# GNN edge and node kernel on one core: the destination rows of a group of 512 edges come as five blocks of 128 rows in one transfer, and five matmuls pick them where eight did

## The reference, cut to what matters

```python
row, col = edge_index[0], edge_index[1]          # src, dst; both of 50000 edges, dst is sorted
edge_input = concatenate([x[row], x[col], edge_attr], axis=-1)   # 128 + 128 + 16 columns
h    = silu(edge_input @ eW1 + eb1)
m_ij = silu(h @ eW2 + eb2)
agg  = segment_sum(m_ij, row, num_segments=50000)
update = silu(concatenate([x, agg], -1) @ nW1 + nb1) @ nW2 + nb2
out  = layernorm(x + (x + update))
```

## Time and profile before

| | |
|---|---|
| median of three runs | 1586.3 us |
| profiled execution: time, span | 1574.37 us, 1572.9 us |
| TensorE / GpSimd / VectorE / ScalarE busy | 77% / 66% / 48% / 29% of the span |
| DMA, mean over the span | 224 GB/s |
| granted TensorE clock, mean | 0.914 of full |

### The profile page before, as it was taken

One profiled execution on the slowest core, in us unless ns is written; L12 is line 12 of the kernel. 1 busy time (PEld: TensorE's weight loads), 2 busy tenths in 40 slices (PEclk: granted clock), 3 DMA queues, 4 the chain that ended last, 5 costly groups with the idle time before them and its releaser, 6 DMA issues.

```text
span 1572.9 us, 24119 instructions
## 1 busy us (share of the span) xinstructions
PE 1207.4 (77%) x6825; PEld 865.5 (55%) x6825; DVE 761.0 (48%) x2819; ACT 459.5 (29%) x846; POOL 1041.8 (66%) x1267
## 2 busy tenths in 40 slices
PE   3812677788787888878888877777778979999994
PEld 3711354555554555545545454544445569888884
DVE  8940343443434434344343333333333449888885
ACT  0000111222222222222222222211212247777774
POOL 8877466556565565555656565666566548999996
PEclk9985799899999999998999898989889889999998
DMA  9995444456666666566656556555545259999994
GB/s 376 410 408 204 123 126 140 145 172 200 183 185 190 186 195 182 186 192 181 192 177 200 170 172 183 172 172 172 165 147 176 62 197 410 412 412 413 410 408 167
DMA packets 175498, 352.94 MB, mean 224 GB/s; under 512 B 30350, under 2 KB 81855, under 8 KB 175364
## 3 DMA queue, kind: packets, MB, share of 16 engines
q1 hardware_dynamic: 128740, 230.97, 44.6%
q10 hardware_dynamic: 21600, 68.32, 10.9%
q0 software_dynamic: 25024, 52.10, 10.5%
HBM read 235.21 MB, written 116.06 MB: 223 GB/s over the span
## 4 chain that ended last, share of the span: by engine, by line
PE 35%; issue 23%; another core or an unknown queue 17%; POOL 12%; DVE 8%; SPq 2%; DMA 2%; POOLq 0%; ACT 0%; DVEq 0%
PE psum L659 10%; POOL windows L614 6%; PE psum L703 5%; PE psum L682 4%; PE psum L705 4%; PE psum L701 3%; PE psum L690 3%; PE psum L715 3%; PE psum L647 2%; DVE same L994 2%; DVE work L988 2%; DVE work L978 2%; POOL windows L594 2%; POOL windows L603 2%
## 5 line engine op out<-in xcount | busy, mean ns | idle before, releaser
L540 POOL DMA_INDIRECT table<-qs,pos x391 | 387.9, 992 | 346.9 <-DVE qs L1022 250.0
L497 POOL DMA_INDIRECT ring<-x_d,idx_src x391 | 397.9, 1018 | 128.0 <-issue 118.5
L659 PE MATMUL psum<-work,windows 128*128 128x128 f32 x1568 | 235.8, 314 | 158.7 <-issue 158.7
L659 PEld LDWEIGHTS psum<-work,windows 128*128 128x128 f32 x1568 | 224.8, 225 | 227.9 <-issue 227.9
L978 DVE COPY work<-psum 128x512 f32<-128x512 f32 x98 | 67.8, 692 | 515.6 <-remote 322.4
L733 PE MATMUL psum<-work,ring 128*128 128x80 f32 x1250 | 156.8, 280 | 27.6 <-DVE work L1042 24.1
L733 PEld LDWEIGHTS psum<-work,ring 128*128 128x128 f32 x1250 | 148.7, 195 | 37.1 <-issue 20.1
L703 PE MATMUL psum<-work,w_src 128*128 128x512 f32 x196 | 117.9, 685 | 48.3 <-DVE work L978 45.5
L1022 DVE COPY qs<-psum 128x512 f32<-128x512 f32 x98 | 67.6, 689 | 161.4 <-remote 150.7
L682 PE MATMUL psum<-xT_in,w_self 128*128 128x320 f32 x314 | 126.5, 487 | 24.8 <-issue 19.1
L785 ACT COPY u_out<-psum 128x320 f32<-128x320 f32 x129 | 55.0, 426 | 295.3 <-remote 250.6
(11 more groups left out here) (121 smaller groups left out, 1613.3 us busy)
## 6 DMA issues: line engine op xcount, KB each, us to landing
windows<-x_d SPq DMA_DIRECT2D x392, 128.0 KB
ring<-table SPq DMA_DIRECT2D x79, 528.0 KB, 11.0
table<-empty ACTq DMA_DIRECT2D x9, 4224.0 KB
edge_rows<-edges_dram SPq DMA_DIRECT2D x98, 384.0 KB
xT_in<-xT_d SPq DMA_DIRECT2D x78, 320.0 KB
out<-windows ACTq DMA_DIRECT2D x78, 320.0 KB, 6.1
u_dram<-u_out SPq DMA_DIRECT2D x64, 320.0 KB
own_x<-x_d SPq DMA_DIRECT2D x48, 320.0 KB, 8.5
```

The lines of the kernel that those rows point to most:

```text
L497: pool.indirect_dma_start(rows, None, x[:, :], bass.IndirectOffsetOnAxis(ap=idx[:, g * TILES + t:g * TILES + t + 1], axis=0)).then_inc(don ...
L540: pool.indirect_dma_start(table[:, :], bass.IndirectOffsetOnAxis(ap=pos[:, g * TILES + t:g * TILES + t + 1], axis=0), q[g % Q][:, t, :], None,
L659: last = nc.tensor.matmul(p_dst[:, t * P:(t + 1) * P], window[g % WINDOWS][:, t, r * D:(r + 1) * D], pick[g % 2][:, r, t * P:(t + 1) * P], ...
```

## The change

Instead of four windows of 256 rows, one for each tile of edges, a group gets one span of 640 rows (SPAN = 5 blocks of 128): tile t's destinations lie in blocks t and t+1. The span comes with one register load and one transfer, row p of block j on partition p, so a piece of 512 B for each partition and block. Matmul j (j in 0..4) multiplies block j with the picks of the tiles that can need it: tiles j-1 and j, 256 columns, at the ends one tile and 128 columns. The two halves of `pick` are stored tile by tile so that these picks are neighbours. The first row is found once for a group, from destinations minus 128 times the tile number. There are four buffers of 5 x 128 values for each partition where there were three of 8 x 128, and the first span is requested ahead of the first edges' numbers. The host hands in a second copy of x with 128 zero rows ahead and 768 behind. The padding edges' destinations run on from 50000 and no longer all name the last row.

```diff
-WINDOWS = 3
+WINDOWS = 4
+SPAN = TILES + 1
+FRONT, BACK = P, SPAN * P

-        windows = sb("windows", [P, WINDOWS * TILES * 2 * D])
-        window = [windows[:, s * TILES * 2 * D:(s + 1) * TILES * 2 * D].rearrange("p (t c) -> p t c", t=TILES)
-                  for s in range(WINDOWS)]
+        windows = sb("windows", [P, WINDOWS * SPAN * D])
+        window = [windows[:, s * SPAN * D:(s + 1) * SPAN * D].rearrange("p (j d) -> p j d", j=SPAN) for s in range(WINDOWS)]

                 wait(sp, s_dst_turned, g - WINDOWS + 1)
-                for t in range(TILES):
-                    at = sp.value_load(first_row[0:1, g * TILES + t:g * TILES + t + 1], min_val=0, max_val=N - WINDOW)
-                    sp.dma_start(window[g % WINDOWS][:, t, :], x[bass.ds(at, WINDOW), :].rearrange("(p r) d -> p (r d)", p=P)
-                                 ).then_inc(s_window[g % WINDOWS], 16)
+                at = sp.value_load(first_row[0:1, g:g + 1], min_val=0, max_val=N + FRONT)
+                sp.dma_start(window[g % WINDOWS], x_wide[bass.ds(at, SPAN * P), :].rearrange("(j p) d -> p j d", p=P)
+                             ).then_inc(s_window[g % WINDOWS], 16)

             with sp.If_eq(sp.to_reg(fit), 1):
+                load_windows(0)
                 for g in range(-3, GROUPS):
                     load_edges(edges_dram[min(g + 3, GROUPS - 1)], g + 3)
-                    load_windows(g + 3)
+                    load_windows(g + WINDOWS)

-            pool.iota(row_i[:], [[1, 2]], base=0, channel_multiplier=2).then_inc(s_iota, 1)
+            pool.iota(row_i[:], [[P, 2]], base=0, channel_multiplier=1).then_inc(s_iota, 1)
+            pool.iota(tile_i[:], [[P, TILES]], base=0, channel_multiplier=0).then_inc(s_tile_i, 1)

-                wait(pe, s_window[g % WINDOWS], 16 * TILES * (g // WINDOWS + 1))
+                wait(pe, s_window[g % WINDOWS], 16 * (g // WINDOWS + 1))
                 wait(pe, s_pick, g + 1)
                 wait(pe, s_xdT, g)
-                for t in range(TILES):
-                    for r in range(2):
-                        last = nc.tensor.matmul(p_dst[:, t * P:(t + 1) * P], window[g % WINDOWS][:, t, r * D:(r + 1) * D],
-                                                pick[g % 2][:, r, t * P:(t + 1) * P], start=r == 0, stop=r == 1)
+                for j in (1, 3, 2, 0, 4):
+                    tiles = slice(max(j - 1, 0) * P, min(j + 1, TILES) * P)
+                    places = slice(max(2 * j - 1, 0) * P, min(2 * j + 1, 2 * TILES) * P)
+                    last = nc.tensor.matmul(p_dst[:, tiles], window[g % WINDOWS][:, j, :], pick[g % 2][:, places],
+                                            start=j == 1, stop=j == 4, skip_group_check=True)

-            V.tensor_reduce(dst_min[:], dst_i[:], AX.X, ALU.min)
-            V.tensor_reduce(dst_max[:], dst_i[:], AX.X, ALU.max).then_inc(s_plan, 1)
+            V.tensor_tensor(dst_rel[:], dst_i[:], tile_i[:].unsqueeze(2).to_broadcast([GROUPS, TILES, P]), ALU.subtract
+                            ).then_inc(s_rel, 1)
+            dve.wait_ge(s_rel, 1)
+            V.tensor_reduce(dst_min[:], dst_rel[:].rearrange("g t p -> g (t p)"), AX.X, ALU.min)
+            V.tensor_reduce(dst_max[:], dst_rel[:].rearrange("g t p -> g (t p)"), AX.X, ALU.max).then_inc(s_plan, 1)
...
-            V.tensor_scalar(dst_first[:], dst_min[:], float(N - WINDOW), None, ALU.min).then_inc(s_plan, 1)
+            V.tensor_scalar(dst_first[:], dst_min[:], -float(FRONT), None, ALU.max).then_inc(s_plan, 1)
...
-            V.tensor_copy(first_i[:], dst_first[:]).then_inc(s_first, 1)
+            V.tensor_scalar(first_i[:], dst_first[:], float(FRONT), None, ALU.add).then_inc(s_first, 1)
+            V.tensor_tensor(below[:], dst_first[:], dst_min[:], ALU.subtract)
...
-            V.tensor_tensor(edges_b[:, 0, :].rearrange("g (t p) -> g t p", p=P), dst_i[:],
-                            dst_first[:].unsqueeze(2).to_broadcast([GROUPS, TILES, P]), ALU.subtract).then_inc(s_edges_b, 1)
+            V.tensor_scalar(edges_b[:, 0, :], dst_rel[:].rearrange("g t p -> g (t p)"), dst_first[:, 0:1], None, ALU.subtract
+                            ).then_inc(s_edges_b, 1)
...
-            V.tensor_copy(part_f[:], slot_i[:, 0:1])
...
-            V.tensor_reduce(worst[0:GROUPS, :], reach[:], AX.X, ALU.max).then_inc(s_plan, 1)
+            V.scalar_tensor_tensor(out=worst[0:GROUPS, :], in0=below[:], scalar=float(WINDOW), in1=reach[:], op0=ALU.mult,
+                                   op1=ALU.max).then_inc(s_plan, 1)

                 for r in range(2):
-                    last = V.tensor_scalar(pick[g % 2][:, r, :], places, row_f[:, r:r + 1], None, ALU.is_equal)
+                    last = V.tensor_scalar(pick[g % 2].rearrange("p (t r e) -> p t r e", t=TILES, r=2)[:, :, r, :],
+                                           places.rearrange("p (t e) -> p t e", t=TILES), row_f[:, r:r + 1], None, ALU.is_equal)
```

More of the change, by code:

```diff
@@ L109, in gnn_kernel @@
         minus_half = sb("minus_half", [P, NODE_ROWS])
[L110 removed]
+        row_f = sb("row_f", [P, 2])
         local_ids = sb("local_ids", [P, BUCKET])
[L112 removed]
+        first_row = sb("first_row", [1, GROUPS], I32)
         idx_src, idx_dst = sb("idx_src", [P, COLS], I32), sb("idx_dst", [P, COLS], I32)
@@ L128, in gnn_kernel @@
         work = sb("work", [P, 12 * GROUP])
-        pick = [work[:, s * 2 * GROUP:(s + 1) * 2 * GROUP].rearrange("p (r e) -> p r e", r=2) for s in range(2)]
+        pick = [work[:, s * 2 * GROUP:(s + 1) * 2 * GROUP] for s in range(2)]
         xsT, xdT, hT, mT = ([work[:, (4 + 2 * k + s) * GROUP:(5 + 2 * k + s) * GROUP] for s in range(2)] for k in range(4))
@@ L156, in gnn_kernel @@
             dst_i = tmp("dst_i", [GROUPS, TILES, P], I32)
-            dst_min, dst_max, dst_first = (tmp(n, [GROUPS, TILES]) for n in ("dst_min", "dst_max", "dst_first"))
-            first_i = tmp("first_i", [GROUPS, TILES], I32)
-            reach, fullest = tmp("reach", [GROUPS, TILES]), tmp("fullest", [P, 1])
+            dst_rel = tmp("dst_rel", [GROUPS, TILES, P])
+            tile_i = tmp("tile_i", [GROUPS, TILES], I32)
+            dst_min, dst_max, dst_first, below = (tmp(n, [GROUPS, 1]) for n in ("dst_min", "dst_max", "dst_first", "below"))
+            first_i = tmp("first_i", [GROUPS, 1], I32)
+            reach, fullest = tmp("reach", [GROUPS, 1]), tmp("fullest", [P, 1])
             worst, worst_all, fits = tmp("worst", [P, 1]), tmp("worst_all", [1, 1]), tmp("fits", [1, 1])
@@ L166, in gnn_kernel @@
         for tile, bytes_in in ((work[:, :].bitcast(F16), 48 * GROUP), (qs[:, :].bitcast(F16), Q * TILES * ROW * 4),
-                               (windows[:, :].bitcast(F16), WINDOWS * TILES * 2 * D * 4), (edge_rows, ROWS_IN * 6 * GROUP),
+                               (windows[:, :].bitcast(F16), WINDOWS * SPAN * D * 4), (edge_rows, ROWS_IN * 6 * GROUP),
                                (own_homes, 4 * CHUNK * COARSES)):
@@ L450, in _ @@
             with sp.Else():
+                pass_on_gathered(0)
                 for g in range(-3, GROUPS):
@@ L453, in _ @@
                     serve_self(g)
-                    pass_on_gathered(g + 3)
+                    pass_on_gathered(g + WINDOWS)
                     if g >= 0:
@@ L490, in _ @@
             pool.iota(slot_i[:], [[0, BUCKETS_IN_BLOCK]], base=0, channel_multiplier=1).then_inc(s_slot_i, 1)
-            pool.iota(row_i[:], [[1, 2]], base=0, channel_multiplier=2).then_inc(s_iota, 1)
-            pool.iota(own_b.rearrange("a k e -> a (k e)"), [[0, 3 * TILES], [2, P]], base=0, channel_multiplier=0,
+            pool.iota(row_i[:], [[P, 2]], base=0, channel_multiplier=1).then_inc(s_iota, 1)
+            pool.iota(tile_i[:], [[P, TILES]], base=0, channel_multiplier=0).then_inc(s_tile_i, 1)
+            pool.iota(own_b.rearrange("a k e -> a (k e)"), [[0, 3 * TILES], [1, P]], base=0, channel_multiplier=0,
                       allow_small_or_imprecise_dtypes=True).then_inc(s_edges_b, 1)
@@ L514, in gather_dst @@
                 for t in range(TILES):
-                    gather(window[g % WINDOWS][:, t, 0:D], idx_dst, g, t, s_dst_gathered[g % WINDOWS])
+                    gather(window[g % WINDOWS][:, t, :], idx_dst, g, t, s_dst_gathered[g % WINDOWS])
             pool.memset(ones[:], 1.0).then_inc(s_consts, 1)
@@ L1100 @@
     arrays = {
-        "x_d": x, "xT_d": by_block(x),
+        "x_d": x, "x_wide_d": np.concatenate([np.zeros((FRONT, D), x.dtype), x, np.zeros((FRONT + BACK, D), x.dtype)]),
+        "xT_d": by_block(x),
         "src_all_d": np.concatenate([by_partition(src_padded), by_group(src_padded)], axis=1),
         "src_idx_d": by_partition(np.concatenate([src, np.zeros(pads, src.dtype)])),
-        "dst_idx_d": by_partition(dst_padded), "dst_g_d": dst_padded.reshape(-1, GROUP),
+        "dst_idx_d": by_partition(dst_padded),
+        "dst_g_d": np.concatenate([dst, np.arange(N, N + pads).astype(dst.dtype)]).reshape(-1, GROUP),
```

13 lines of the change are left out of this document (7 added, 6 removed).

## The result

Timed against each other, the changed kernel took 1571.24 us (20 runs) and the kernel before 1580.97 us (20 runs): ratio 0.9933, 95% interval 0.9912 to 0.9955. So 0.7% faster, about 10 us, where 29 were forecast. The profiled execution took 1559.37 us, against 1574.37 before; its span is 15.0 us shorter. It is the fastest of the twenty, so the 15 us are more than the medians' 10. A hand-over is the news of a finished instruction that reaches the engine waiting for it; it comes as a change of a semaphore.

What follows compares the result with a forecast made beforehand. The kernel was taken to be bound by waits along GpSimd, hand-over, VectorE, GpSimd. Start 15, loop 11 and matmuls 3, less 0.1, gave 29 us: median 1586.3 to 1557, range 1505 to 1595.

Steps and rivals of the forecast that it cites:

- The start: Start of the edge loop: SyncE silent, hand-overs 4 us apart, first scatter near 168 us; 15 us gained, bounds 0 and 25.
- Two signs: At the start: first scatter near 168 not 181.35 us if right; ScalarE's longest wait well under 24 us.
- The loop: Long groups with gathers: fewer SyncE issues let some hand-overs come 1.5 us earlier; 11 us gained, bounds 0 and 53.
- Matmuls: Destination matmuls, eight become five: 0.1 us saved in each of 28 groups without gathers, 3 us; bounds 0 and 8.
- The transfer: Window loads: 1.57 us of all DMA engines a group becomes 1.08, hidden by early requests, so worth nothing.
- the picks: VectorE's L988 writes the same 512 values in four runs of 128: no change; bounds 0 and 11 us.
- the plan: One more VectorE pass at startup, about 0.5 us, covered by startup gathers; GpSimd's added iota costs 0.12 us.
- the 1.2 us allowed: Startup: first edge numbers come one span, 1.2 us, later, covered by ScalarE's fill until 106.4 us.
- Hand-overs do not care about SyncE: Rival, 27%: SyncE's issues do not affect hand-overs; only the matmuls' 3 us remain, 1583 us, between 1578 and 1589.
- The burst: Rival, 17% with slower picks: packets at once delay hand-overs 0.69 us in 70 long groups, 48 us; 1631 us.

Runs made afterwards that it cites:

- second pair: Changed kernel and kernel before, both run again unchanged on another late chip: 1571.11 us beside 1581.11, ratio 0.994.
- padded kernels: Changed kernel plus a GpSimd memset after each gather and scatter; late chips: 0.9867 of the kernel before at 1.39 us pace, 0.9917 at 1.60.
- four-issue kernel: Changed kernel with its span brought by four issues, same bytes and matmuls: late chip 1587.21 us beside 1590.75, ratio 0.998; prompt chips 1.0008 and 1.001.

## Why the prediction was wrong

**The direction and what bounds the kernel** were right. The path GpSimd, hand-over, VectorE, GpSimd is what the late chips show. Where news is prompt the same code takes 1343 us, 238 less.

**The start (15 of the 29 us) is the step that failed.** As put: SyncE falls silent, so the hand-overs at the start come 4 us apart and the first scatter near 168 us. SyncE did fall silent, though from 133.5 us and not from about 93, and GpSimd's stall did vanish, but the first scatter came at 178.63: 2.7 us gained, and in the second pair 2.6. I had read the 23 us as caused by SyncE's issues because both stood in the same stretch. ScalarE's 27.41 us ran on through 24 us of silence, so the issues do not cause them. The padded kernels show that GpSimd's pace does, on a late chip: with 1.60 us between gathers the copy comes at 130.9. Whether four issues would be short at that pace was not run. With the stall gone, GpSimd issued the same gathers earlier and stood for 10.5 us behind them; that a longer backlog is the reason is argued. Two signs that I had named came out against it: the first scatter stayed near 181, and ScalarE's longest wait at the start was 27.41 us and not well under 24. Before, the longest had been 27.32 us (L774, until 171.53), not the 24.08 of the earlier trace rows, so the wait had not changed at all.

**The loop (11 us)** was nearly right: 16.3 us in the profiled pair, 8.6 in the second. The four-issue kernel supports that it hangs on the issues, as put, with the reservations above. So does the place of the gain: more copies come amid the gathers, as the prediction had it for some groups. The size came out of two estimates (1.5 us, a third of the groups) and may be luck. That issues and news share what the backlog holds up is argued, not shown.

**Matmuls (3 us).** Ten instructions took 1.90 us at full clock, where sixteen took 1.95:

```profile
188.28 1.90 PE L667 MATMUL psum<-work,windows 128*128 128x256 f32 x10
```

0.05 us, 28 times, is 1.4 us and not 3. At half clock the ten took 3.75 us, as the sixteen had the earlier trace rows, so the 0.2 us taken there were nothing:

```profile
151.88 3.75 PE L667 MATMUL psum<-work,windows 128*128 128x256 f32 x10 [8.17 <-issue]
```

The 0.15 us that came, as an estimate, from the Trainium skill, TensorE: Matmul & The Clock Gate, section Back-to-back issue gap, did not show at full clock. Eight matmuls in place of five changed nothing on a prompt chip; on a late one this was not measured.

**The transfer, the picks and the plan** at nothing: the DMA share fell to 0.54 over the stretch of the earlier trace rows, and the four-issue kernel, with a share of 0.52, stands only 0.2% under the kernel before. Picks did not get slower (L1001 has a median of 487 ns, as L988 had). The first edge numbers came later than the 1.2 us allowed: SyncE's issues of them took up to 9.4 us behind the spans. On a late chip that is covered; whether it is part of the 3 us lost on a prompt one is open.

**The rivals.** "Hand-overs do not care about SyncE" was right about the start and, as far as the four-issue kernel shows, wrong about the loop. The Trainium skill, DMA: Bandwidth & Descriptors, section Issuing engines are not separate DMA queues, holds issuing to be small beside the transfer: on prompt chips the runs agree (four issues 1.0008 and 1.001, one 1.002), on late ones three more issues in a group cost some 0.4%, and four at the start took 25.25 us. The burst did not come; with it the time would have grown.

**The sum.** It gave 29 us. In the two profiled pairs start and loop brought 19.0 and 11.2 us, and the stage after the loop took 3.9 and 1.3 back, which no step of mine foresaw; the timed medians differ by 10. So 19 us of the 29 were missing, and 12 of them are the start's. The forecast of 1557 was off by 14 only, since the median of three runs that it started from, 1586.3, lay 5 above that of twenty.

## What to carry to other kernels

When waits end at no instruction's end, look at the engine that issues indirect transfers, and ask at what pace it issues them; an experiment that slows the issuer a little tells more than one that takes work away. Before believing a gain of under 1%, run both kernels on more than one chip: here the same change is 0.7% faster on one kind and 0.2% slower on the other, and a padding that wins 1.3% on the one loses 6% on the other. A stall that is taken from such an engine may only move: here 9.19 us amid the gathers became 10.5 us behind them.

## What the runs showed of the hardware

- The same program takes 1343 us on some chips and 1581 to 1591 us on others, with nothing between in eight comparisons. What the traces show to differ is the hand-over of TensorE's news while GpSimd issues gathers and scatters: no wait named remote in any trace from a prompt chip, 836 to 1111 us of them in the two kernels on late ones.
- GpSimd can issue a gather of 128 rows of 512 B every 1.25 us and a scatter every 1.28. On late chips the news of finished matmuls then comes late, at the start by up to 48 us (in the kernel before L659 ended at 123.18 and ScalarE's copy of its result started at 171.53). At 1.39 us between them it is still late, and at 1.60 us no wait is named remote.
- Scatters count as well as gathers: with gathers 2.56 us apart and scatters between them the news was still up to 7.3 us late in the stretch shown.
- SyncE's issues are long on the same chips: the same four took 25.25 us on a late one and at most 9.46 on a prompt one.
